# Layer 2 of a two-layer network: attention and routing batch by batch, whole rows scattered to the experts' lists

## The reference, cut to what matters

```python
def _L1_xattn_ref(q, k, v):
    scaled = jnp.einsum('bsd,bse->bde', q, k) * scale
    attn = jax.nn.softmax(scaled, axis=1)
    return jnp.einsum('bde,bse->bsd', attn, v)

def _L1_ffn_ref(x, router_w, expert_bias, gate_proj, up_proj, down_proj):   # 16 experts, 4 chosen, 224 inner
    logits = jnp.einsum('bsh,eh->bse', x, router_w) + expert_bias
    scores = jax.nn.softmax(logits, axis=-1)
    top_w, top_idx = jax.lax.top_k(scores, TOP_K)
    top_w = top_w / jnp.sum(top_w, axis=-1, keepdims=True)
    act = jax.nn.silu(x @ gate_proj) * (x @ up_proj)                          # for each expert
    ... # sum of the chosen experts' act @ down_proj, weighted with top_w

x = x + _L0_ffn_ref(_layernorm(x), ...)
x = x + _L1_xattn_ref(_layernorm(x), ctx_2048, ctx_2048)
x = x + _L1_ffn_ref(_layernorm(x), ...)
```

## Time and profile before

| | us |
|---|---|
| median of 3 runs | 775.46 |
| lowest and highest of them | 774.98, 780.38 |
| time of the profiled execution | 776.06 |
| its span in the profile | 774.3 |
| attention and routing of layer 2, from the first load to the next stage | 458.59 to 593.22 |
| the tile stage, to the next one | 593.22 to 752.44 |
| the last stage | 752.44 to 774.3 |

### The profile page before, as it was taken

The page is one execution under the profiler, slowest core; times in us unless marked ns, Lnnn a source line. Parts: engine busy times, 40 slices in busy tenths (PEclk is TensorE's granted clock), DMA queues, the critical chain, the costliest instruction groups (busy, mean ns, idle before and its releaser), DMA issues. The chain is left out here.

```text
span 774.3 us, 11100 instructions
## 1 busy us (share of the span) xinstructions
PE 477.6 (62%) x3303; PEld 360.8 (47%) x3303; DVE 380.1 (49%) x1226; ACT 207.7 (27%) x533; POOL 340.2 (44%) x464
## 2 busy tenths in 40 slices
PE   1715976887784209987899703254500889899920
PEld 1611533444442108876688602233400888888810
DVE  8955555888854503533344405878640123222217
ACT  0540453555563104322233201021100222222200
POOL 9483210555554533644455510030552566666510
PEclk9965897999977558999999955565655799999965
DMA  5199896764889638899954239100034499999716
GB/s 164 54 197 302 319 294 178 200 168 138 264 287 348 235 119 261 273 331 302 305 183 158 78 115 402 62 1 21 21 88 136 128 294 291 287 294 291 235 46 252
DMA packets 83086, 157.18 MB, mean 203 GB/s; under 512 B 12523, under 2 KB 53493, under 8 KB 81248
## 3 DMA queue, kind: packets, MB, share of 16 engines
q1 hardware_dynamic: 54928, 91.89, 37.7%
q10 hardware_dynamic: 14944, 32.71, 13.5%
q0 software_dynamic: 13168, 32.02, 12.4%
HBM read 102.95 MB, written 56.12 MB: 205 GB/s over the span
## 5 line engine op out<-in xcount | busy, mean ns | idle before, releaser
L1140 DVE TENSOR_REDUCE at_top<-at_ps_top 128x2 f32<-128x512 f32 x128 | 83.5, 685 | 50.7 <-PE at_ps_top L1051 49.7
L1514 POOL DMA_INDIRECT rows<-hd_out,hd_rows x64 | 62.2, 972 | 68.6 <-DVE hd_out L1465 45.9
L1367 PE MATMUL hd_ps_up<-hd_x_turned,e_arena 128*128 128x160 f32 x512 | 84.8, 310 | 0.0
L1213 ACT ACTIVATE at_prob<-at_ps_score 128x512 f32<-128x512 f32 x128 | 71.6, 593 | 44.8 <-PE at_ps_score L1069 44.3
L1672 PE MATMUL l_ps_up<-l_x_turned,e_up_w 128*112 128x128 f32 x672 | 82.8, 278 | 0.0
L1672 PEld LDWEIGHTS l_ps_up<-l_x_turned,e_up_w 128*112 128x112 f32 x672 | 81.6, 182 | 2.6
L1367 PEld LDWEIGHTS hd_ps_up<-hd_x_turned,e_arena 128*128 128x128 f32 x512 | 78.2, 197 | 8.9 <-issue 6.2
L845 POOL DMA_INDIRECT held<-e_extended,e_address x64 | 62.8, 980 | 34.3 <-issue 18.9
L642 POOL DMA_INDIRECT table<-choice,ft_r_address x32 | 30.6, 957 | 104.4 <-DVE ft_r_address L633 95.6
L1051 PE MATMUL at_ps_top<-e_arena 96*128 96x256 bf16 x256 | 57.0, 312 | 26.4 <-PEq L110 21.7
L1502 DVE TENSOR_TENSOR hd_inner<-hd_silu,hd_ps_up 128x160 f32<-128x160 f32 x64 | 20.5, 321 | 77.9 <-ACT hd_silu L1452 77.9
(11 more groups left out here) (277 smaller groups left out, 867.3 us busy)
## 6 DMA issues: line engine op xcount, KB each, us to landing
e_up_w<-in_up SPq DMA_DIRECT2D x42, 448.0 KB, 4.5
held<-e_empty ACTq DMA_DIRECT2D x16, 960.0 KB, 6.9
e_arena<-in_weights ACTq DMA_DIRECT2D x32, 384.0 KB, 5.1
e_arena<-in_weights SPq DMA_DIRECT2D x32, 384.0 KB, 11.7
hd_rows<-held SPq DMA_DIRECT2D x15, 768.0 KB, 10.8
e_down_w<-in_down SPq DMA_DIRECT2D x42, 224.0 KB, 5.6
ft_g_rows<-rows SPq DMA_DIRECT2D x8, 1024.0 KB, 10.9
parts<-op_parts SPq DMA_DIRECT2D x8, 576.0 KB, 6.5
```

Source lines behind the costliest of these rows:

```text
L1140: nc.vector.reduce_max(top[:, 2 * h:2 * h + 2], ps_top[at % TOPS][:], AX_X).then_inc(top_found, 1)
L1213: nc.scalar.activation(prob[at % RING][:], ps_score[at % SCORES][:], ACT.Exp, scale=scale).then_inc(prob_ready, 1)
L1367: op = nc.tensor.matmul(ps_up[e % 2][:, part, :], w[:, k, part * P:(part + 1) * P], x_turned[g % 2][:, j, k, :], start=k == 0, stop=k == 1)
L1514: nc.gpsimd.indirect_dma_start(rows_out, to, out_ap, None, bounds_check=TOKENS * LAYER0.chosen - 1, oob_is_err=False).then_inc(semaphore, 16)
```

## The change

Layer 2 gets the lists of whole rows that layer 1 has, and `features_phase` goes over single batches.

- `features_phase`: ten steps. In step t batch t is normed, scored and attended, batch t-1 gets its second norm, is turned, scored by the router and chosen, batch t-2 its targets, places and four scatters of 128 rows of 1152 B each. VectorE adds all eight expert rows and x (`halve`); one identity matmul (`add_rows`) puts the sum in PSUM, and the attention accumulates on it there. The first norm's scale is computed by GpSimd (`pool_scale`, with a power and two Newton steps), the second's by VectorE (`dve_scale`); both are applied by ScalarE, which also copies x back. The look-ups are replaced by the scan and the maximum of `RowRouting`. The plan stands ahead of the last batch's targets and places.
- `tiles_phase`: in place of the gather GpSimd clears the places beyond the end of a tile's list (an indirect scatter of a fill, with the valid rows out of bounds), and SP loads the tile's rows directly once the clear has landed, ahead of the tile's weights. VectorE takes weight and target from the rows (`pick`, with a register load) and multiplies the output with the weight. Output rows of unused places are dropped by the bounds check.
- `last_phase`: the rows come weighted, VectorE adds four and x by halving, one batch at a time.
- The table, its zeroing, the lists, the spare rows and the store of normalised rows are gone. In layer 1 a few waits are added (`known`, `ready`, `expo_ready`, `weights_ready`).

The diff, cut to its core:

```diff
+    def pool_scale(self, pool, link, b):
+
+        nc, (full, square, work) = self.nc, (self.work[:, k:k + 1] for k in range(3))
+        root, shift = self.scale[:, b % 2, 0:1], self.scale[:, b % 2, 1:2]
+        pool.wait_ge(self.known, b + 1)
+        link(nc.gpsimd.tensor_scalar(full, self.mean_var[:, 1:2], EPS, None, ALU.add))
+        link(nc.gpsimd.tensor_tensor(root, full, self.power[:], ALU.pow))
+        for _ in range(NEWTON - 1):
+            link(nc.gpsimd.tensor_tensor(square, root, root, ALU.mult))
+            link(nc.gpsimd.tensor_scalar(work, square, full, -0.5, ALU.mult, ALU.mult))
+            link(nc.gpsimd.tensor_scalar(root, work, 1.5, root, ALU.add, ALU.mult))
+        nc.gpsimd.tensor_scalar(shift, self.mean_var[:, 0:1], root, -1.0, ALU.mult, ALU.mult).then_inc(self.ready, 1)
+
+    def act_apply(self, act, b, to, x, normed):
+        act.wait_ge(self.ready, b + 1)
+        self.nc.scalar.activation(to, x, ACT.Identity, bias=self.scale[:, b % 2, 1:2], scale=self.scale[:, b % 2, 0:1])\
+            .then_inc(normed, 1)
...
         dve.wait_ge(self.expo_ready, b + 1)
+        if self.spare:
+            link(self.nc.vector.scalar_tensor_tensor(self.junk[:], self.expo[:], 1.0, self.held.mask[:, b, :], ALU.mult, ALU.mult,
+                                                     accum_out=self.total[:]))
...
+            def load_rows(i, u):
+                c = sp.value_load(experts.tile_column[0:1, bass.ds(i * U + u, 1)], min_val=0, max_val=layer.columns)
+                sp.wait_ge(cleared[u], i * 16 + 16)
+                sp.dma_start(rows[u][:], by_tile[bass.ds(c, 1)].rearrange("a p n -> (a p) n")).then_inc(rows_loaded[u], 16)
+
+            sp.wait_ge(experts.scattered, 16 * layer.chosen * B)
             last = groups(sp)
-
+            for u in range(U):
+                load_rows(0, u)
             with sp.Fori(1, last + 1) as i:
...
+                    load_rows(i, u)
                     experts.load(sp, i, u)
...
+            def clear(i, u):
+                c = pool.value_load(experts.tile_column[0:1, bass.ds(i * U + u, 1)], min_val=0, max_val=layer.columns)
+                nc.gpsimd.tensor_copy(index[u][:], experts.clear_rows[:, bass.ds(c, 1)]).then_inc(index_ready, 1)
+                pool.wait_ge(index_ready, i * U + u + 1)
+                pool.sem_inc(parted, 1)
+                to = bass.IndirectOffsetOnAxis(ap=index[u][:], axis=0)
+                nc.gpsimd.indirect_dma_start(listed_dram, to, empty[:], None, bounds_check=E * TOKENS + P - 1,
+                                             oob_is_err=False).then_inc(cleared[u], 16)
 
             def scatter(i, u):
-
                 to = bass.IndirectOffsetOnAxis(ap=target[u][:], axis=0)
-                nc.gpsimd.indirect_dma_start(rows_out, to, out[u][:], None).then_inc(stored[u], 16)
+                nc.gpsimd.indirect_dma_start(rows_out, to, out[u][:], None, bounds_check=TOKENS * layer.chosen - 1,
+                                             oob_is_err=False).then_inc(stored[u], 16)
...
+                    pool.wait_ge(out_kept, i * U + u - U + 1)
+                    pool.sem_inc(parted, 1)
+                    pool.wait_ge(cleared[u], i * 16)
+                    pool.sem_inc(parted, 1)
+                    clear(i, u)
+                    scatter(i - 1, u)
...
+            def pick(i, u, free):
+                e = dve.value_load(experts.tile_expert[0:1, bass.ds(i * U + u, 1)], min_val=0, max_val=E - 1)
                 if not free:
-                    dve.wait_ge(stored[u], i * 16 + (0 if layer.by_token else 16))
+                    dve.wait_ge(stored[u], i * 16)
+                nc.vector.tensor_copy(weight[u][:], rows[u][:, bass.ds(e * 2 + D, 1)])
+                nc.vector.tensor_copy(target[u][:], rows[u].bitcast(I32)[:, bass.ds(e * 2 + (D + 1), 1)])
+
+            def keep(i, u):
                 dve.wait_ge(down_done, i * U + u + 1)
-                if layer.by_token:
-                    nc.vector.tensor_copy(target[u][:], column[u][:, 0, 1:2])
-                nc.vector.tensor_copy(out[u][:], ps_out[u % 2][:]).then_inc(out_kept, 1)
+                nc.vector.tensor_scalar(out[u][:], ps_out[u % 2][:], weight[u][:], None, ALU.mult).then_inc(out_kept, 1)
...
+            for b in range(B):
+                sp.dma_start(rows[b][:], by_batch[b]).then_inc(rows_loaded[b], 16)
+                if b == 0:
+                    sp.dma_start(keys[:], ctx.rearrange("b p n -> p b n")).then_inc(inputs_loaded, 16)
+                    sp.dma_start(vals[:], ctx_turned.rearrange("b p k n -> p b k n")).then_inc(inputs_loaded, 16)
+                    sp.dma_start(gate[:], gate_dram).then_inc(inputs_loaded, 16)
+                    sp.dma_start(gate_bias[:], gate_bias_dram).then_inc(inputs_loaded, 16)
             experts.load_first(sp, plan.planned)
...
+            first.pool_start(link)
+            for t in STEPS:
+                if t < B:
+                    first.pool_scale(pool, link, t)
+                if t >= 2:
+                    for k in range(layer.chosen):
+                        routing.pool_scatter(pool, t - 2, k)
...
+            def add_rows(b):
+                pe.wait_ge(halved, b + 1)
+                if b >= 2:
+                    pe.wait_ge(x_kept, b - 1)
+                    pe.wait_ge(routing.normed, b - 1)
+                nc.tensor.matmul(ps_x[b % 2][:], consts.identity[:], rows[b][:, 0, :], start=True, stop=True).then_inc(summed, 1)
+
+            def score(b):
+                if b == 0:
+                    pe.wait_ge(inputs_loaded, 64)
+                pe.wait_ge(normed, b + 1)
+                if b >= 2:
+                    pe.wait_ge(expo_ready, b - 1)
+                for c in range(2):
+                    op = nc.tensor.matmul(ps_scores[b % 2][:, c, :], keys[:, b, c * P:(c + 1) * P], x_norm[b % 2][:], start=True, stop=True)
+                op.then_inc(scored, 1)
+
+            def attend(b):
+                pe.wait_ge(vals_ready, b + 1)
+                for c in range(2):
+                    op = nc.tensor.matmul(ps_x[b % 2][:], vals_shared[b % 2][:, c, :], expo[b % 2][:, c, :], start=False, stop=c == 1,
+                                          skip_group_check=True)
+                op.then_inc(attended, 1)
+
+            add_rows(0)
+            for t in STEPS:
+                if 1 <= t <= B:
+                    routing.pe_turn(pe, t - 1)
+                if t < B:
+                    score(t)
+                if 1 <= t <= B:
+                    routing.pe_score(pe, t - 1)
+                if t + 1 < B:
+                    add_rows(t + 1)
+                if 1 <= t <= B:
+                    routing.pe_rank(pe, t - 1)
+                if t < B:
+                    attend(t)
+                if t == B:
+                    plan.pe_count(pe)
...
+            for t in STEPS:
+                if t < B:
+                    first.act_apply(act, t, x_norm[t % 2][:], ps_x[t % 2][:], normed)
+                if 1 <= t <= B:
+                    b = t - 1
+                    routing.act_normalise(act, b, ps_x[b % 2][:], second)
+                    nc.scalar.activation(x_all[:, b, :], ps_x[b % 2][:], ACT.Copy).then_inc(x_kept, 1)
+                    routing.act_keep_turned(act, b)
...
+                if t >= 2:
+                    routing.act_weights(act, t - 2)
...
+            def halve(b):
+                dve.wait_ge(rows_loaded[b], 16)
+                width = HALF
+                while width >= 1:
+                    link(nc.vector.tensor_tensor(rows[b][:, 0:width, :], rows[b][:, 0:width, :], rows[b][:, width:2 * width, :], ALU.add))
+                    width //= 2
+                nc.vector.tensor_tensor(rows[b][:, 0, :], rows[b][:, 0, :], x_all[:, b, :], ALU.add).then_inc(halved, 1)
...
+            halve(0)
+            for t in STEPS:
+                if t < B:
+                    dve.wait_ge(summed, t + 1)
+                    first.dve_stats(dve, link, t, ps_x[t % 2][:])
+                if 1 <= t <= B:
+                    dve.wait_ge(attended, t)
+                    second.dve_stats(dve, link, t - 1, ps_x[(t - 1) % 2][:])
+                    second.dve_scale(dve, link, t - 1)
+                if t >= 2:
+                    routing.dve_targets(dve, link, t - 2)
+                    routing.dve_places(dve, link, t - 2)
+                if t < B:
+                    dve.wait_ge(scored, t + 1)
+                    link(nc.vector.reduce_max(top[:], ps_scores[t % 2][:], AX_X))
+                    nc.vector.tensor_scalar(minus_top[t % 2][:], top[:], -scale, None, ALU.mult).then_inc(top_known, 1)
+                if t + 1 < B:
+                    halve(t + 1)
+                if 1 <= t <= B:
+                    if t == 1:
...
+                    routing.dve_choose(dve, link, t - 1)
+                if t < B:
+                    dve.wait_ge(expo_ready, t + 1)
+                    nc.vector.reciprocal(share[t % 2][:], total[t % 2][:]).then_inc(share_ready, 1)
```

(20 more changed lines are left out.)

698 lines of the change are left out of this document (200 added, 498 removed).

## The result

| | before | after |
|---|---|---|
| median of the runs | 775.22 us (4 runs, 774.66 to 780.38) | 802.29 us (4 runs, 801.4 to 803.11) |
| ratio to before, 95% interval | | 1.0317 (1.028 to 1.0355) |
| span of the profiled execution | 774.3 us | 801.3 us |
| mean granted TensorE clock | 0.801 | 0.787 |
| first halving add of the stage of layer 2 | 463.60 | 465.97 |

The kernel is 3.2% slower, 27 us. The predicted time (804) is 1.7 us off. Most of the 27 us, 21.2, is in the loop: its last turn follows the first by 153.2 us, where it was 132.0. The first turn comes 8.1 us later than before, and what stands behind the last turn is 2.3 us shorter.

What follows compares the result with a forecast made beforehand. GpSimd's indirect DMAs were taken to pace the tile loop before the change. The terms 12.4 + 0.85 + 16.7 + 0.6 - 2.2 = 28.4 us gave span 802.7 and time 804 us, range 785 to 826.

Steps and rivals of the forecast that it cites:

- Part 1: Stage of layer 2 by single batches: a chain of 14.2 us a step, with the stage's end +12.4 us.
- The cover for GpSimd's norm: Stage of layer 2: GpSimd's first norm, 2.8 us, stays off the chain if its pow takes under 2 us.
- The end of the stage: Stage of layer 2: planned at 588.5, then SP's twelve weight transfers, 9.4 us, are late next, ending at 598.8.
- The change of stage: From SP's end at 598.8 to the expert stage of layer 2: 6.8 us, so it starts at 605.6.
- Part 3: Tile loop: a cycle through clear and row load of 11.0 us for three tiles, 3.67 a tile, +16.7 us.
- The two unknown landings: Tile loop: middles of ranges taken, 3.85 us for the clear and 3.45 for the row load.
- Quiet* (A): Tile loop rival: clear and load land as in an idle machine, 5.1 us together; 789 us, chance 0.14.
- Loaded* (C): Tile loop rival: both landings at the medians, 5.0 + 4.5 us, 4.4 a tile; 832 us, chance 0.12.
- Rival B: Stage of layer 2 bound by VectorE's work, steps falling toward 10.0 us; 775 us, chance 0.11.
- Tail and last stage: VectorE's extra work at the loop's end +0.6 us; last stage by halving one batch at a time -2.2 us.
- The first layer: Layer 1: the added waits cost nothing, as the new semaphores count events a batch old.

Runs made afterwards that it cites:

- experiment 6: Kernel after, with the halving of the next batch moved into VectorE's two waits of a step in the stage of layer 2: ratio 1.0185.
- experiment 7: Kernel after, with TensorE doing the scores of batch t ahead of the transposes of batch t-1: ratio 1.0314.
- experiment 10: The edits of experiment 1, experiment 4, experiment 6 and experiment 8 together, plus TensorE's order of experiment 7: ratio 0.9989.
- experiment 11: The edits of experiment 1, experiment 4, experiment 6 and experiment 8 together, plus ScalarE's gate weights right behind the step's first apply: 764.14 us, ratio 0.984.
- experiment 8: Kernel after, with the weights of four of six tiles issued in the next stage, each behind its tile's row load: ratio 1.0215.
- experiment 1: Kernel after, with each clear issued three tiles ahead and after the scatter that shared its turn: ratio 1.0045.
- experiment 2: Kernel after, with only the scatter put in front of the clear and nothing issued ahead: ratio 1.0472.
- experiment 3: Kernel of experiment 1, with the clear one tile ahead instead of three: ratio 1.0170.
- experiment 4: Kernel of experiment 1, with the copy of the clear's indices ahead of the wait and the scatter: ratio 1.0003.

## Why the prediction was right

The mechanism is the forecast one in each stage. That the total is off by only 1.7 us is in part luck: the first turn came 5.2 us sooner than forecast and the loop took 4.5 us more, and two smaller misses cancel in part.

- **The steps (Part 1).** Forecast 14.2 us, measured 13.38; from share(0) to share(7) 91.3 us for 96.6. The chain is the one laid out, and VectorE waits where it was said to (4.2 us a step on the scores and on attend, as forecast, and 0.3 more on the identity matmul). The link most overpriced is the one from the transposes to the maximum, 503.04 - 500.60 = 2.44 for 2.77: the scores' matmul begins 0.48 us after the transposes do, inside their 0.69. Choosing, up to the share, took 1.04 (506.62 to 507.66) for 1.29, the row maximum and its small one 0.80 for 0.90, the hand-offs less than allowed for. The start up to share(0) went the other way, 14.7 us for 14.0, all of it GpSimd's norm. One reading was wrong without consequence: before the change VectorE is not nearly always busy in this stage, but 7.72 of 14 us in the window cited the earlier trace rows and 79 of 108 us from 464 to 572.
- **The cover for GpSimd's norm.** Forecast 2.8 us and a pow of less than 2 us. Measured 3.3 (508.76 to 512.03 on GpSimd); the pow (L541) takes 0.57. In the kernel after the cover holds: ScalarE applies at 512.07, and VectorE's scale for the other norm comes later. But it holds by little. The scatters that should start 7 us into a step and take 5.0 start 8.4 in and take 5.7, and the norm's first instruction finds GpSimd idle for 0.35 us only:

```profile
508.76 0.24 POOL L540 TENSOR_SCALAR ft_n_work<-ft_n_mean_var 128x1 f32<-128x1 f32 x1 [0.35 <-DVE ft_n_mean_var L516]
```

  Experiments 6, 7, 10 and 11 show how near it was: any edit that makes a step shorter, or the scatters later, makes GpSimd the bound.
- **The end of the stage.** From share(7) to the plan 14.2 us for 14.4, and SP's twelve transfers from 586.91 to 596.59, 9.7 for 9.4. That SP is late next was right: experiment 8. The change of stage was priced too high. In the rows of after, by start time on GpSimd, SP and TensorE:

```profile
602.15 0.34 POOL L1445 MEMSET l_empty<- 128x288 f32 x1 [9.73 <-POOLq L104]
604.28 0.99 POOL L1454 DMA_INDIRECT listed<-l_empty,l_index  x1 [0.90 <-POOL l_index L1450]
606.58 3.05 SPq L1429 DMA_DIRECT2D l_rows<-listed  x2
608.77 0.69 PE L1495 MATMUL l_ps_x<-identity,l_rows 128*128 128x128 f32 x2 [23.75 <-DMA l_rows<-listed]
```

  Counted back from the clear by the forecast's own 3.1, the stage starts at 601.2, 4.6 us behind SP and not 6.8. (Over the kernels with the same order of loads, 3.1 to 6.1 us pass from SP's last issue to GpSimd's fill, which is 5.6 here, so that this is one draw of a length that varies.) The first turn comes 7.6 us later for 8.35: SP goes 2.3 us after the clear's issue (2.85 forecast), and its load lands in 2.2 (2.4). First turn forecast at 613.95, measured at 608.77, of which the late start of the stage is 2.4 the other way.
- **The loop (Part 3).** The mechanism was right, and experiments 1 to 3 show it. The first turn to the last took 153.2 us for 148.7. The largest mis-sized term is the first of the cycle, the 3.57 from turn to issue read off one round at the loop's start: measured 2.04 + 1.11 + 1.08 = 4.23. The two unknown landings came out well: clear to row load 4.12 for 4.0 together with the hand-off, row load to turn 3.09 for 3.45. In sum 11.44 for 11.0 a round. The 35 tiles behind the seventh turn took 135.1 us for 128.5; the seventh turn itself came 18.1 us after the first for 20.2, which takes 2.1 back.
- **The landings' rivals.** *Quiet* (A) is out, though its reason was right: the skipped rows move next to nothing, and the clear takes a median of 3.4 us all the same, for the 2.7 of the shortest gather. *Loaded* (C) did not occur in this kernel, but experiment 3 came near it as soon as the loop ran faster (4.8 and 3.7 us). The page "DMA: Bandwidth & Descriptors" of the Trainium skill (the anatomy of one DMA) would have kept the loop at GpSimd's pace, by an estimate of 4.7 us for clear and row load together. The page gives that price for DMAs that GpSimd issues, as the clear is; the row load is SP's. The 7.2 us from the clear's issue to the turn, and the 21 us of experiment 1, are against that estimate here.
- **Rival B**, a stage at VectorE's own work, did not occur in the kernel after. Experiment 6 fills the waits and comes within 1.6 us of the 10.0 before GpSimd stops it.
- **Tail and last stage.** Last turn to last scatter +1.1 for +0.6; from there to the end 28.2 us for 31.6, so -3.4 for -2.2.
- **The first layer** was costed at nothing, and the stage starts 2.4 us later. 1.8 of it is there at the reciprocal of layer 1 named above, which starts at other times from trace to trace; it is not shown to be the change's.

The sum: forecast 28.4; first turn 5.2 sooner, loop 4.5 more, tail 0.5 more, end 1.2 less gives 27.0.

## What to carry to other kernels

Replacing a lookup that one DMA does by a clear and a load in series keeps the number of GpSimd's DMAs, gives SP one more a tile and adds a landing to a loop-carried cycle: count the cycle over its number of tiles in flight, and put the DMA that depends on nothing as far ahead as its buffers allow (three tiles gave all, one gave half). A loop held up by a cycle of latencies shows landings shorter than it will have when it runs faster, so take landings at the load of the loop you aim at. When the DMA share nears 1, look also at the pace of the queue that issues the loads. Before shortening one engine's step, look for the closed round of the next engine: here GpSimd's norm, the gap to its scatters and the scatters. My reordering of TensorE lengthened that gap in both kernels that had it.

## What the runs showed that I had not expected

- An ALU.pow of one column on GpSimd took 0.57 us, about twice a plain tensor_scalar there (0.24 to 0.27).
- The landing of the same 144 KB row load had a median of 2.8 us at 251 GB/s and 4.4 at 274 GB/s (of 5 landings); the clear, which moves next to nothing, 3.4 and 4.8.
- SP's three loads a tile followed each other in 2.95 us at the shortest in experiment 4, and there its row loads waited for nothing else.
- GpSimd's small norm instruction took 0.24 us in experiments 6, 7 and 10, and 1.01 in 11 (0.78 a round earlier), directly behind an indirect DMA in all of them.
